# Moving the first pass over a quantised block from ScalarE to VectorE, with new orders for all engines

## The chip, the cores and the metric

The kernel runs on one core of a Trainium2 chip. Time is device time in microseconds (us). The engines are TensorE (PE in the rows), VectorE (DVE), ScalarE (ACT), GpSimd (POOL), and SyncE (SP), which only issues DMAs here. A repeated run of this kernel gave 1418.02 to 1421.85 us.

## The reference

x is (4, 2048, 512) in f32, the context (4, 77, 512). What is computed, cut to what matters:

```python
x = x + tanh(g_xattn[0]) * xattn(layernorm(x), ctx, ctx, mask, Wq, Wk, Wv, Wo)   # 16 heads of 32, 77 keys
x = x + tanh(g_ffn[0]) * ffn(layernorm(x), w_gate, w_up, w_down)                 # 512 -> 2048 -> 512

def act_quant(x):      # per token
    scale = 127.0 / clip(max(abs(x), axis=-1), 1e-5)
    return clip(round(x * scale), -128, 127) / scale
def weight_quant(w):   # ternary
    scale = 1.0 / clip(mean(abs(w)), 1e-5)
    return clip(round(w * scale), -1, 1) / scale
def bitlinear(x, w): return act_quant(x) @ weight_quant(w).T
ffn = lambda x: bitlinear(silu(bitlinear(x, w_gate)) * bitlinear(x, w_up), w_down)
```

## The kernel before

The 8192 tokens are worked on in 16 blocks of 512, each of four tiles of 128. Work is cut into pieces with names such as `F:gu12`: a part (the letter), a step, a tile (or half) and a number in it. The parts run side by side on different blocks. In a repeated round for block g, `A` is the attention of block g, `N` and `Q` are the first layer norm and the q product of block g+1, `F` is the feed-forward net of block g-1, and `E` the end of that of g-2. `W` is the preparation of the weights, in the front alone, with `M` and `R` for block 0's norm and q.

The order of the pieces on each engine is written out by hand in strings: `TENSOR_`, `SCALAR_`, `VECTOR_`, `POOL_` and `SYNC_`, each with `_FIRST` (the front), `_ORDER` (the repeated round) and `_LAST` (the end). `turn` walks through a string and calls the piece's function. Each engine runs its pieces strictly in that order, and semaphores between engines do the rest. So a piece that waits holds up all that stands behind it on its engine.

The feed-forward net for a tile t, step by step:

- `gu` on TensorE (line 1199): gate and up product for one of four column blocks of 512 into two banks; on ScalarE a tanh of the gate (line 739); on VectorE (1 + tanh) times the gate (line 1014); on GpSimd that times `up` (line 607). `up` on ScalarE copies the up product out of its bank (line 747).
- `hm` on VectorE: the largest magnitude of a column block (line 1020). `hs`: six operations on 128x1 that make the scales (lines 1027 to 1032).
- `hq` (line 751, ScalarE): the first pass over the 128x2048 tile, times the scale plus a large number, which rounds. `hb` (line 757, ScalarE): the second pass, minus that number, to bf16. `tH` on the queue of SyncE transposes it by DMA, and `down` on TensorE (line 1211) multiplies it; `down` on VectorE (line 1038) adds x, and a bank is free again.

In the attention, `sc` on TensorE (line 1142) gives scores of five row groups per half; ScalarE takes the exponential twice, to f32 and f16 (lines 707, 708), and GpSimd their difference, the low part (line 598). `pv` (lines 1163 to 1166) is the product with the values, `al` and `ah` the split of it, `wo` (lines 1069 to 1071) the output product, `st`, `zn`, `za` the second layer norm and its scale, `l1` and `l2` its newton steps on GpSimd (lines 563 to 569). In `N`, `xn` normalises (line 938) and `xl` makes the low part (line 943); in `Q`, `q` is the product and its split (line 947 the low part), `s` the maxima of a head's scores (lines 1115 and 953), `mT` their transpose, and `m` on the queue the mask and maxima rows that the scores need.

In `W`, `ws` sums magnitudes on ScalarE, `wm` reduces them over partitions on GpSimd (line 573) and makes the mean, `wu` and `wc` on VectorE clip and round a 128x2048 quarter (lines 913, 919), `wt` on ScalarE writes it as ternary. `w` on the queue loads the next matrix into the quarter that `wt` has read. There are three matrices with four quarters each. The second layer norm's tile lies where the quarters lay, so `A:zn00` waits for all twelve.

Of the kernel before, what the change touches and what calls it, by code (L numbers as in the profile page):

```python
# [11 lines left out]
TT = GT // P  # L12
# [18 lines left out]
def spans(c):  # L31
# [17 lines left out]
MAGIC = 1.5 * 2.0 ** 23  # L49
# [11 lines left out]
    F:gu00 F:gu01 F:gu02 A:sc00 A:sc01 F:gu03 F:gu10 A:sc02 E:down30 A:sc03 A:sc04 F:gu11 F:gu12 A:sc10 F:gu13  # L61
    A:pv00 A:pv01 A:sc11 F:gu20 A:sc12 A:pv02 A:sc13 F:down00 A:sc14 A:pv03 F:gu21 F:gu22 A:pv10 A:pv11 F:gu23
    A:pv12 A:pv13 F:gu30 A:wo00 A:wo10 Q:q00 Q:q10 Q:q20 Q:q30 A:wo20 Q:s00 F:down10 Q:s01 A:wo30 Q:s10 F:gu31
# [3 lines left out]
    F:gu00 E:hq30 F:up00 F:gu01 E:hb30 F:up01 F:gu02 F:up02 F:gu03 A:sc00 F:up03 F:gu10 A:sc01 F:up10 A:sc02  # L67
    F:hq00 A:sc03 F:gu11 A:sc04 F:up11 F:gu12 F:hb00 F:up12 F:gu13 A:sc10 A:sc11 A:ah00 A:ah01 F:up13 A:sc12
    F:gu20 A:ah02 N:xh00 A:sc13 A:sc14 N:xh10 F:up20 F:gu21 A:ah03 F:gu22 F:up21 A:ah10 F:gu23 F:up22 N:xh20
    A:ah11 N:xh30 A:ah12 F:hq10 Q:q00 F:hb10 F:gu30 Q:q10 F:up23 F:up30 A:ah13 A:zq00 A:zb00 Q:q20 Q:q30 A:zq10  # L70
    F:hq20 F:hb20 F:gu31 F:up31 A:zb10 A:zq20 A:zb20 F:gu32 F:gu33 F:up32 F:up33 A:zq30 A:zb30 Q:mT00
"""
VECTOR_ORDER = """
    F:gu00 F:gu01 F:hm00 F:gu02 F:gu03 F:hm01 F:hm02 F:hm03 F:gu10 F:hs00 E:down30 F:gu11 F:gu12 N:ln00 A:pv00
    A:pv01 F:gu13 A:al00 A:al01 N:xn00 N:xn10 A:pv02 F:gu20 F:hm10 F:down00 A:al02 F:hm11 A:pv03 N:xl00 N:xl10
    F:gu21 A:al03 A:pv10 A:pv11 A:al10 F:hm12 N:xn20 F:gu22 N:xl20 A:al11 N:xn30 A:pv12 N:xl30 A:al12 F:hm13
    F:hs10 A:wo00 A:pv13 F:gu23 A:st00 F:hm20 F:hm21 A:wo10 A:st10 Q:q00 F:hm22 A:zn00 A:za00 Q:q10 F:hm23
    F:hs20 Q:q20 A:zn10 Q:q30 F:gu30 A:al13 A:za10 A:wo20 A:st20 Q:s00 F:hm30 F:down10 Q:s01 A:zn20 A:za20
    A:wo30 Q:s10 A:st30 Q:s11 F:gu31 Q:s20 F:gu32 A:zn30 F:gu33 Q:s21 Q:s30 F:hm31 A:za30 F:hm32 Q:s31 Q:mh00
    F:hm33 F:hs30 F:down20  # L80
# [106 lines left out]
def gated_cross_attention_and_ternary_ffn(nc, x, ctx4, mask_keys, mask_cols, mask_rows, gates, wqT, wkT, wvT, woT,  # L187
# [3 lines left out]
    ALU, ACT, AX = mybir.AluOpType, mybir.ActivationFunctionType, mybir.AxisListType  # L191
# [6 lines left out]
    with ctx:  # L198
# [48 lines left out]
        h = region[:, 0:2 * FF].rearrange("p (u n) -> p u n", u=2)  # L247
        hT = region[:, 2 * FF:3 * FF].bitcast(bf16).rearrange("p (u k n) -> p u k n", u=2, k=FK)

        hb = sb("hb", [P, FF], bf16)  # L250
# [1038 lines left out]
```

## Time and profile before

| | |
|---|---|
| median of 3 runs | 1420.9 us (1418.02 to 1421.85) |
| the profiled execution | 1424.24 us, span 1422.4 us, mean granted clock of TensorE 0.958 |
| TensorE busy | 1294.4 us (91%) |
| VectorE busy | 1122.4 us (79%) |
| ScalarE busy | 971.0 us (68%) |
| GpSimd busy | 718.3 us (50%) |

The profiled execution is one of its own, so sums made from its trace are made against its time. An engine's busy time is a mean over stages; the stages here are the front (no feed-forward product yet, to 154.5 us), the repeated rounds, and the end from 1297 us.

### The profile page before, as it was taken

How to read it: one execution, taken by the hardware profiler on the slowest of the kernel's cores; microseconds unless marked ns; L12 is line 12 of the kernel's file. 1: busy time of each engine (PE TensorE's matmuls, PEld its weight loads, DVE VectorE, ACT ScalarE, POOL GpSimd, SP SyncE). 2: the span in 40 equal slices, each digit the busy share in tenths (PEclk: the TensorE clock that was granted, in tenths of full speed). 3: DMA queues.
4: the chain of work that ended last, by engine and by line, in shares of the span. 5: the costliest groups of instructions: out<-in, count | busy, mean ns of one | idle time of the engine just before them, and what ended most of it. 6: DMA issues, size and time to landing. Idle time of an engine off the chain costs nothing.

```text
span 1422.4 us, 25997 instructions
## 1 busy us (share of the span) xinstructions
PE 1294.4 (91%) x7424; PEld 636.9 (45%) x7998; DVE 1122.4 (79%) x2577; ACT 971.0 (68%) x1404; POOL 718.3 (50%) x1187
## 2 busy tenths in 40 slices
PE   5748899999999999999999999999999999999996
PEld 2214344545444454544444454544445454444542
DVE  6978588887968697796969789696878879697784
ACT  4765666768586766858576675958667585857874
POOL 2033354647364563746455464735546473645552
PEclk8867899999999999999999999999999999999999
DMA  8763446464553637354463636346463644536332
GB/s 303 238 205 76 117 86 159 101 150 108 137 132 85 161 83 166 92 150 106 97 173 85 166 92 152 99 112 154 84 164 100 151 104 124 131 81 152 76 77 78
DMA packets 386616, 181.63 MB, mean 128 GB/s; under 512 B 324147, under 2 KB 357811, under 8 KB 384947
## 3 DMA queue, kind: packets, MB, share of 16 engines
q1 hardware_dynamic: 386560, 181.04, 50.8%
q14 instruction: 40, 0.33, 0.1%
q8 instruction: 16, 0.26, 0.1%
HBM read 61.64 MB, written 35.46 MB: 68 GB/s over the span
## 4 chain that ended last, share of the span: by engine, by line
PE 42%; DVE 26%; issue 11%; ACT 9%; POOL 6%; DMA 4%; SPq 1%; ACTq 0%; POOLq 0%; DVEq 0%
PE bank L1211 11%; PE bank L1199 9%; PE bank L1069 7%; PE bank L1070 6%; PE bank L1071 6%; DVE xh L943 4%; DVE xn L938 4%; DVE nmax L953 3%; DVE hmx L1020 2%; ACT up L747 2%; DMA xT<-xh 2%; POOL region L607 2%; DVE region L1014 2%; DVE ah L977 2%; DVE at L971 2%
## 5 line engine op out<-in xcount | busy, mean ns | idle before, releaser
L607 POOL TENSOR_TENSOR region<-region,up 128x512 f32<-128x512 f32 x256 | 336.4, 1322 | 236.7 <-ACT up L747 133.5
L1014 DVE SCALAR_TENSOR_TENSOR region<-region,bank 128x512 f32<-128x512 f32 x256 | 174.4, 682 | 149.2 <-ACT region L739 148.9
L1199 PE MATMUL bank<-tern_gate,region 128*128 128x512 fp8e4 x1024 | 264.5, 381 | 23.5 <-DVE o L1038 14.4
L1199 PE MATMUL bank<-tern_up,region 128*128 128x512 fp8e4 x1024 | 263.2, 379 | 0.0
L1211 PE MATMUL bank<-tern_down,region 128*128 128x512 fp8e4 x1024 | 252.4, 404 | 8.2 <-DMA region<-hb 6.3
L598 POOL TENSOR_TENSOR work<-work 124x512 f16<-124x512 f32 x160 | 195.7, 1237 | 34.3 <-ACT work L708 34.3
L739 ACT ACTIVATE region<-bank,fs 128x512 f32<-128x512 f32 x256 | 180.3, 706 | 47.4 <-PE bank L1199 45.1
L1020 DVE TENSOR_REDUCE hmx<-region 128x1 f32<-128x512 f32 x256 | 170.6, 677 | 38.7 <-POOL region L607 37.8
L751 ACT ACTIVATE region<-region,fs 128x2048 f32<-128x2048 f32 x64 | 127.8, 1996 | 52.5 <-DVE fs L1031 52.5
L1211 PEld LDWEIGHTS bank<-tern_down,region 128*128 128x128 bf16 x1024 | 103.7, 103 | 123.9 <-issue 28.1
L747 ACT ACTIVATE up<-bank 128x512 f32<-128x512 f32 x256 | 154.7, 618 | 4.2 <-PE bank L1199 3.8
L563 POOL TENSOR_TENSOR rs<-mv,lnc 128x1 f32<-128x1 f32 (+1 forms) x80 | 15.3, 192 | 236.5 <-DVE mv L988 220.2
L1199 PEld LDWEIGHTS bank<-tern_up,region 128*128 128x128 bf16 x1024 | 99.0, 97 | 78.7 <-issue 1.1
L757 ACT ACTIVATE hb<-region 128x2048 bf16<-128x2048 f32 x64 | 122.8, 1918 | 0.8 <-DMA region<-hb 0.4
L1199 PEld LDWEIGHTS bank<-tern_gate,region 128*128 128x128 bf16 x1024 | 91.6, 97 | 70.1 <-issue 0.5
L1142 PE MATMUL bank<-q_stack,k_stack 128*128 128x512 f16 x384 | 107.3, 388 | 16.1 <-DMA q_stack<-mT 8.4
L707 ACT ACTIVATE work<-bank,con 124x512 f32<-124x512 f32 x160 | 116.1, 725 | 7.2 <-PE bank L1142 4.4
L708 ACT ACTIVATE work<-bank,con 124x512 f16<-124x512 f32 x160 | 117.3, 733 | 0.0
L953 DVE TENSOR_REDUCE nmax<-bank 128x4 f32<-128x308 f32 x256 | 109.8, 468 | 3.9 <-PE bank L1115 3.3
L722 ACT ACTIVATE region<-region,fs 128x512 f32<-128x512 f32 x64 | 46.2, 723 | 93.8 <-DVE fs L1007 93.7
L1069 PE MATMUL bank<-xT,wq_hi 128*128 128x512 f16 x256 | 97.8, 382 | 9.6 <-DMA xT<-xh 6.9
L1069 PE MATMUL bank<-wo_hi,aT 128*128 128x512 f16 x256 | 98.2, 384 | 6.2 <-issue 5.0
(142 smaller groups left out, 2447.1 us busy)
## 6 DMA issues: line engine op xcount, KB each, us to landing
q_stack<-q_rows SPq DMA_DIRECT2D x96, 256.0 KB, 5.1
xbig<-in_x SPq DMA_DIRECT2D x16, 1024.0 KB, 5.4
q_rows<-q SPq DMA_DIRECT2D x64, 256.0 KB, 2.8
out_y<-o SPq DMA_DIRECT2D x64, 256.0 KB, 2.6
q_stack<-mT SPq DMA_DIRECT2D x32, 256.0 KB, 4.0
region<-in_wgT SPq DMA_DIRECT2D x4, 1024.0 KB, 14.0
region<-in_wuT SPq DMA_DIRECT2D x4, 1024.0 KB, 6.4
region<-in_wdT SPq DMA_DIRECT2D x4, 1024.0 KB, 5.8
```

What stands on the lines that cost most here:

```text
L598: nc.gpsimd.tensor_tensor(p_lo[0:CR, at, :], p32[0:CR, at % PSLOTS, :], p_hi[0:CR, at, :], ALU.subtract).then_inc(p_lo_ready, 1)
L607: nc.gpsimd.tensor_tensor(ht, ht, up[:, n % 2, :], ALU.mult).then_inc(hmul_ready, 1)
L739: nc.scalar.activation(h[:, t % 2, n * GT:(n + 1) * GT], pb[2 * (n % 2)][:, :], ACT.Tanh, scale=fs[:, t, CG:CG + 1]).then_inc(tanh_ready, 1)
L747: nc.scalar.activation(up[:, n % 2, :], pb[2 * (n % 2) + 1][:, :], ACT.Copy).then_inc(up_ready, 1)
L751: nc.scalar.activation(h[:, t % 2, :], h[:, t % 2, :], ACT.Copy, bias=MAGIC, scale=fs[:, t, HSC:HSC + 1]).then_inc(hq_ready, 1)
L757: nc.scalar.activation(hb[:, :], h[:, t % 2, :], ACT.Copy, bias=-MAGIC).then_inc(hb_ready, 1)
L953: V.tensor_reduce(nmax[:, t, HC * cc:HC * (cc + 1)], pb[6 + cc % 2][:, 0:SROWS].rearrange("p (h n) -> p h n", h=HC), AX.X, ALU.max, negate ...
L1014: V.scalar_tensor_tensor(ht, ht, 1.0, pb[2 * (n % 2)][:, :], ALU.add, ALU.mult).then_inc(silu_ready, 1)
L1020: V.tensor_reduce(hmx[:, t % 2, n:n + 1], ht, AX.X, ALU.max, apply_absolute_value=True).then_inc(hmax_ready, 1)
L1069: T.matmul(dst, a_hi_, b_hi_, start=first, stop=False)
L1199: ins = T.matmul(pb[2 * (n % 2) + w][:, :], xqT[:, k, tok], tern[w][:, k * FF + n * GT:k * FF + (n + 1) * GT], start=(k == 0), stop=(k == ...
L1211: ins = T.matmul(pb[2][:, :], hT[:, t % 2, k, :], tern[2][:, k * GT:(k + 1) * GT], start=(k == 0), stop=(k == FK - 1))
```

## The change

The first pass `hq` moves from ScalarE to VectorE: one `tensor_scalar` with multiply and add instead of one activation. Its wait stays the same one, for the scale, and its reader `hb` stays on ScalarE. All 15 order strings are written anew. They were made under the rule that VectorE's two-operand work and GpSimd exclude each other. All other functions stay as they are. The code and, of the strings, the first line of the repeated round of two engines:

```diff
-SCALAR_ORDER = """
-    F:gu00 E:hq30 F:up00 F:gu01 E:hb30 F:up01 F:gu02 F:up02 F:gu03 A:sc00 F:up03 F:gu10 A:sc01 F:up10 A:sc02
+SCALAR_ORDER = """
+    F:gu00 F:up00 E:hb30 F:gu01 F:up01 F:up02 F:gu02 A:sc00 A:sc01 F:gu03 A:sc02 F:gu10 F:up03 A:sc03 A:sc04
-VECTOR_ORDER = """
-    F:gu00 F:gu01 F:hm00 F:gu02 F:gu03 F:hm01 F:hm02 F:hm03 F:gu10 F:hs00 E:down30 F:gu11 F:gu12 N:ln00 A:pv00
+VECTOR_ORDER = """
+    E:hq30 F:gu00 F:gu01 F:hm00 F:gu02 F:hm01 F:hm02 F:gu03 F:hm03 F:gu10 F:hs00 E:down30 F:hq00 A:pv00 A:pv01
...
                     act.wait_ge(hmul_ready, k - 2)
                 nc.scalar.activation(up[:, n % 2, :], pb[2 * (n % 2) + 1][:, :], ACT.Copy).then_inc(up_ready, 1)
-            def hq(f, t, _):
-                act.wait_ge(hscale_ready, f * TT + (t + 1))
-                nc.scalar.activation(h[:, t % 2, :], h[:, t % 2, :], ACT.Copy, bias=MAGIC,
-                                     scale=fs[:, t, HSC:HSC + 1]).then_inc(hq_ready, 1)
-
             def h_integers(f, t, _):
                 act.wait_ge(hq_ready, f * TT + (t + 1))
                 act.wait_ge(hT_in[(t + 1) % 2], f * 32 + 16 * ((t + 1) // 2) + 16)
                 nc.scalar.activation(hb[:, :], h[:, t % 2, :], ACT.Copy, bias=-MAGIC).then_inc(hb_ready, 1)
             pieces = {"Q": {"q": q, "mT": m_high}, "A": {"sc": sc, "ah": a_high, "zq": z_quant, "zb": z_integers}, "N": {"xh": x_high},
-                      "F": {"gu": gu, "up": up_copy, "hq": hq, "hb": h_integers},
+                      "F": {"gu": gu, "up": up_copy, "hb": h_integers},
                       "W": {"tn": gates_tanh, "oh": head_rows, "wh": projection_high, "kh": key_high, "vh": value_high,
                             "ws": weight_sum, "wt": weight_ternary}}
             pieces["M"], pieces["R"] = pieces["N"], pieces.get("Q")
...
                 V.tensor_tensor(at(HSC), at(HRC), at(KAP), ALU.mult).then_inc(hscale_ready, 1)
                 V.tensor_tensor(at(HOUT), at(HAQ), c(OUT0), ALU.mult).then_inc(hout_ready, 1)
+            def hq(f, t, _):
+                dve.wait_ge(hscale_ready, f * TT + (t + 1))
+                V.tensor_scalar(h[:, t % 2, :], h[:, t % 2, :], fs[:, t, HSC:HSC + 1], MAGIC, ALU.mult, ALU.add).then_inc(hq_ready, 1)
+
             def output(f, t, _):
                 dve.wait_ge(hout_ready, f * TT + (t + 1))
                 dve.wait_ge(down_mm, f * TT + (t + 1))
...
                       "A": {"pv": normalise, "al": a_low,
                             "wo": residual, "st": ln2_tile, "zn": z_norm_tile, "za": z_amax},
                       "N": {"ln": ln1, "xn": norm_tile, "xl": x_low},
-                      "F": {"gu": gu, "hm": h_amax, "hs": h_scale, "down": output},
+                      "F": {"gu": gu, "hm": h_amax, "hs": h_scale, "hq": hq, "down": output},
                       "W": {"hc": clear_scalars, "hd": masks, "wx": projection_max, "wp": projection_scale, "wl": projection_low, "km": keys_masked,
                             "kp": key_scale, "kc": key_low, "vm": values_masked, "vp": value_scale, "vc": value_low,
                             "es": score_scale, "ys": output_scale, "wm": weight_mean, "wu": weight_upper, "wc": weight_lower}}
```

The queue's string in the front moves too: block 0's x is the first transfer instead of the eighth, block 1's x is sent before any ternary matrix, and the third matrix (`w20` to `w23`) stands behind `R:m00` instead of ahead of it. On TensorE the front's end is now `q`, `wo` and `s` in turns instead of all `wo`, all `q`, all `s`.

Three places in detail. First GpSimd in the front, from the first reduction on, before. A row `ISA` with no operands is a change of the loaded GpSimd code; with `con<-con` it is a reduction over partitions.

```order
L545 ISA
L545 ISA con<-con 128x1 [waits wmax_ready]
L549 ISA con<-con 128x1 [waits kmax_ready]
L573 ISA con<-con 128x1 [waits wsum_ready]
L553 ISA con<-con 128x1 [waits vmax_ready]
L545 ISA con<-con 128x1 [waits wmax_ready]
L573 ISA con<-con 128x1 [waits wsum_ready] x2
L563 ISA
L563 TENSOR_TENSOR rs<-mv,lnc 128x4 [waits ln1_stats]
```

And now the piece from the last reduction of the first group (line numbers are the same here):

```order
L573 ISA con<-con 128x1 [waits wsum_ready]
L563 ISA
L563 TENSOR_TENSOR rs<-mv,lnc 128x4 [waits ln1_stats]
...
L569 TENSOR_TENSOR rs<-rs 128x4 [waits rstd1_step]
L573 ISA
L573 ISA con<-con 128x1 [waits wsum_ready]
L598 ISA
L598 TENSOR_TENSOR work<-work 124x512 [waits p_hi_ready,exp_ready] x10
L573 ISA
L573 ISA con<-con 128x1 [waits wsum_ready]
L563 ISA
```

Before, the reductions of all three matrices stood in one piece, so the code was changed twice. Now the second block's newton steps stand between the first and the second mean, the ten low parts of p between the second and the third, and the code is changed six times.

Second, VectorE at the end of the front, before: the q product's low parts, then all the maxima, then their split for the transpose.

```order
L996 TENSOR_SCALAR region<-xbig,mv,rs 128x512 [waits zb_ready,ln2_rstd]
L1004 TENSOR_REDUCE fs<-region 128x1 [waits z_norm]
L1005 TENSOR_SCALAR fs<-fs 128x1 [waits dve_quant]
L1007 RECIPROCAL fs<-fs 128x1 [waits ln2_scale]
L947 SCALAR_TENSOR_TENSOR q<-bank,q 128x512 [waits q_hi_ready] x2
L953 TENSOR_REDUCE nmax<-bank 128x4 [waits s_mm] x16
L963 TENSOR_SCALAR mhl<-nmax 128x4x16 [waits mT_mm,smax_ready]
L964 SCALAR_TENSOR_TENSOR mhl<-nmax,mhl 128x4x16 [waits dve_loop]
L1014 SCALAR_TENSOR_TENSOR region<-region,bank 128x512 [waits tanh_ready] x2
```

And now, from the third low part of q on (line numbers are lower by 5 here: 948 is 953 of before, 976 is 981):

```order
L942 SCALAR_TENSOR_TENSOR q<-bank,q 128x512 [waits q_hi_ready]
L914 TENSOR_SCALAR region<-region 128x2048 [waits wupper_ready]
L942 SCALAR_TENSOR_TENSOR q<-bank,q 128x512 [waits q_hi_ready]
L980 BN_STATS st<-xbig 128x6 [waits x2_ready]
L982 MEMSET con 128x1 [waits ln2_halves]
L983 BN_AGGR mv<-st 128x2
L976 SCALAR_TENSOR_TENSOR xbig<-bank,con,xbig 128x512 [waits wo_mm]
L948 TENSOR_REDUCE nmax<-bank 128x4 [waits s_mm] x2
L972 TENSOR_TENSOR ah<-at,ah 128x256 [waits ah_ready]
L980 BN_STATS st<-xbig 128x6 [waits x2_ready]
L982 MEMSET con 128x1 [waits ln2_halves]
L983 BN_AGGR mv<-st 128x2
```

The maxima (`nmax`) now stand two at a time between output products' residuals (`xbig<-bank`), statistics and the last rounds of the weights, and 10 of the 24 passes `wu` and `wc` stand behind the first `pv` where 3 did.

Third, VectorE from the end of one round into the next, before: scales and output of the last tile but one, then the gate products and maxima of the next block.

```order
L1031 TENSOR_TENSOR fs<-fs 128x1 [waits dve_ffn]
L1032 TENSOR_TENSOR fs<-fs,con 128x1
L1038 SCALAR_TENSOR_TENSOR o<-bank,fs,xbig 128x512 [waits out_free0,down_mm,hout_ready]
L1014 SCALAR_TENSOR_TENSOR region<-region,bank 128x512 [waits tanh_ready] x2
L1020 TENSOR_REDUCE hmx<-region 128x1 [waits hmul_ready]
L1014 SCALAR_TENSOR_TENSOR region<-region,bank 128x512 [waits tanh_ready] x2
L1020 TENSOR_REDUCE hmx<-region 128x1 [waits hmul_ready] x3
L1014 SCALAR_TENSOR_TENSOR region<-region,bank 128x512 [waits tanh_ready]
L1027 TENSOR_REDUCE fs<-hmx 128x1 [waits hmax_ready,ffn_scalars]
```

And now:

```order
L1026 TENSOR_TENSOR fs<-fs 128x1 [waits dve_ffn]
L1027 TENSOR_TENSOR fs<-fs,con 128x1
L1037 SCALAR_TENSOR_TENSOR o<-bank,fs,xbig 128x512 [waits out_free0,down_mm,hout_ready]
L1031 TENSOR_SCALAR region<-region,fs 128x2048 [waits hscale_ready]
L1009 SCALAR_TENSOR_TENSOR region<-region,bank 128x512 [waits tanh_ready] x2
L1015 TENSOR_REDUCE hmx<-region 128x1 [waits hmul_ready]
L1009 SCALAR_TENSOR_TENSOR region<-region,bank 128x512 [waits tanh_ready]
L1015 TENSOR_REDUCE hmx<-region 128x1 [waits hmul_ready] x2
L1009 SCALAR_TENSOR_TENSOR region<-region,bank 128x512 [waits tanh_ready]
L1015 TENSOR_REDUCE hmx<-region 128x1 [waits hmul_ready]
L1009 SCALAR_TENSOR_TENSOR region<-region,bank 128x512 [waits tanh_ready]
```

The pass `region<-region,fs` is new at the head of the round, directly ahead of the first gate product. A second one stands behind the next tile's scales and output. The other two of a round stand ahead of the first and behind the last low part of q.

## Rows read from the trace of the kernel before

**Rows 1.** The page: busy us (share of the span) xinstructions; TensorE in 40 slices.

```profile
PE 1294.4 (91%) x7424; PEld 636.9 (45%) x7998; DVE 1122.4 (79%) x2577; ACT 971.0 (68%) x1404; POOL 718.3 (50%) x1187
PE   5748899999999999999999999999999999999996
```

**Rows 2.** Busy time by stage; last, one repeated block. Columns as in the first line.

```profile
core 0: us, PE busy (x) PEld busy (x) DVE busy (x) ACT busy (x) POOL busy (x), PEclk, DMA share, GB/s
0.00:154.50 154.50, 96.36 (x401) 42.77 (x403) 121.94 (x231) 85.10 (x97) 38.82 (x83) 0.76 0.67 206
154.50:1297.00 1142.50, 1086.15 (x6417) 539.65 (x6916) 920.82 (x2164) 796.51 (x1188) 618.24 (x1019) 0.98 0.51 123
1297.00:1422.00 125.00, 111.86 (x609) 54.50 (x680) 79.66 (x183) 89.42 (x119) 61.27 (x85) 0.97 0.32 78
...
915.30:997.04 81.74, 78.17 (x462) 38.81 (x497) 65.92 (x155) 57.11 (x87) 44.24 (x74) 0.98 0.51 123
```

**Rows 3.** What TensorE waited for, 915.30 to 997.04 us: us, times, longest.

```profile
PE bank L1115 <- DVE nmax L953: 1.3, 2, 1.1
PE bank L1199 <- DVE o L1038: 0.9, 1, 0.9
PE bank L1199 <- DVE region L1014: 0.6, 2, 0.4
PE bank L1069 <- DMA xT<-xh: 0.4, 1, 0.4
```

**Rows 4.** TensorE around the last maxima: start us, us, engine, operation.

```profile
881.88 0.69 PE L1115 MATMUL bank<-k_max,q 128*128 128x308 f16 x2 [1.13 <-DVE nmax L953]
883.36 5.31 PE L1211 MATMUL bank<-tern_down,region 128*128 128x512 fp8e4 x16
...
899.29 3.62 PE L1211 MATMUL bank<-tern_down,region 128*128 128x512 fp8e4 x16
```

**Rows 5.** The chain of waits, longest pieces: first and last slow down product.

```profile
474.25 5.22 PE bank L1211 x16
...
1292.88 5.21 PE bank L1211 x16
```

**Rows 6.** Groups by line and form: busy us, mean ns, idle before, releaser.

```profile
L607 POOL TENSOR_TENSOR region<-region,up 128x512 f32<-128x512 f32 x256 | 336.4, 1322 | 236.7 <-ACT up L747 133.5 <-DVE region L1014 101.7 <-ACT work L708 1.4
...
L751 ACT ACTIVATE region<-region,fs 128x2048 f32<-128x2048 f32 x64 | 127.8, 1996 | 52.5 <-DVE fs L1031 52.5
...
L943 DVE TENSOR_TENSOR xh<-xn,xh 128x512 f16<-128x512 f32 x64 | 73.6, 1167 | 4.4 <-ACT xh L680 2.6
```

**Rows 7.** VectorE in order of time: rounds alone, with GpSimd busy; a low part alone.

```profile
34.08 1.28 DVE L913 TENSOR_SCALAR region<-region,con 128x2048 f32<-128x2048 f32 x1
35.27 1.22 DVE L919 TENSOR_SCALAR region<-region 128x2048 f32<-128x2048 f32 x1
...
100.10 4.27 DVE L913 TENSOR_SCALAR region<-region,con 128x2048 f32<-128x2048 f32 x2
...
850.33 0.69 DVE L943 TENSOR_TENSOR xh<-xn,xh 128x512 f16<-128x512 f32 x1
```

**Rows 8.** VectorE at the start of a block.

```profile
893.47 0.69 DVE L1014 SCALAR_TENSOR_TENSOR region<-region,bank 128x512 f32<-128x512 f32 x1 [2.27 <-ACT region L739]
...
896.34 0.69 DVE L1014 SCALAR_TENSOR_TENSOR region<-region,bank 128x512 f32<-128x512 f32 x1 [1.34 <-ACT region L739]
```

**Rows 9.** VectorE in the front.

```profile
12.92 2.47 DVE L925 BATCH_NORM_STATS2 st<-xbig 128x6 f32<-128x512 f32 x4 [0.26 <-DMA xbig<-in_x]
...
95.45 1.35 DVE L938 TENSOR_SCALAR xn<-xbig,mv,rs 128x512 f32<-128x512 f32 x1 [7.44 <-POOL rs L569]
...
145.41 7.99 DVE L953 TENSOR_REDUCE nmax<-bank 128x4 f32<-128x308 f32 x16
```

**Rows 10.** TensorE, the first scores.

```profile
88.35 3.40 PE L1142 MATMUL bank<-q_stack,k_stack 128*128 128x512 f16 x7 [7.88 <-DMA q_stack<-mT]
```

**Rows 11.** GpSimd in the front: first reduction, first newton step behind the reductions.

```profile
24.73 0.66 POOL L545 PARTITION_ALL_REDUCE con<-con  x1 [6.07 <-issue]
...
92.69 0.19 POOL L563 TENSOR_TENSOR rs<-mv,lnc 128x4 f32<-128x4 f32 x1 [6.97 <-issue]
```

**Rows 12.** ScalarE at the end: the last first pass and the last second pass.

```profile
1405.95 2.00 ACT L751 ACTIVATE region<-region,fs 128x2048 f32<-128x2048 f32 x1 [1.46 <-DVE fs L1031]
1408.32 1.91 ACT L757 ACTIVATE hb<-region 128x2048 bf16<-128x2048 f32 x1 [0.36 <-DMA region<-hb]
```

## What I expected before the change was run

> **What bounds the kernel now.** I read the page first (busy time by engine, the 40 slices), then busy time by stage, then what TensorE waits for in one repeated block, then single instructions around the longest of those waits. TensorE is busy 91% of the span and 9 tenths or more in nearly every slice but the first four [rows 1]. By stage [rows 2]: up to 154.5 us, where the first feed-forward product starts, it is busy 96.4 us, so 58.1 us are idle; from there to 1297 us it is busy 1086.2 of 1142.5, 56.3 idle; in the last 125 us, 13.1 idle. The middle is fourteen blocks of 512 tokens, about 81.7 us each. In one of them TensorE is busy 78.17, VectorE 65.92, ScalarE 57.11 and GpSimd 44.24 of 81.74 us [rows 2]. So the middle is TensorE's, with at most 81.74 - 78.17 = 3.6 us to win per block, and the front belongs to the other engines and the queue. TensorE's named waits in that block are 1.3 (the maxima), 0.9 (the output that empties a bank), 0.6 (the gate product) and 0.4 us (a transpose): 3.2 us [rows 3]. Where it waits for the maxima it stands 1.13 us, and behind that the `down` product takes 5.31 us instead of 3.62: its clock is at the lower of its two levels there, 1.2 GHz and not 2.4 [rows 4], which costs 1.7 us. The chain of waits shows such a `down` of 5.2 us in eleven of the fourteen blocks, the first at 474.25 and the last at 1292.88 [rows 5].
>
> **The change, part by part.** My sum is made against the profiled execution, 1424.24 us with a span of 1422.4; the median of the runs shown is 1420.9, 3.3 less, so I take every term off the median.
>
> *The first pass.* Line 751 leaves ScalarE: 64 times 1996 ns, 8.0 us per block [rows 6]. VectorE gets 64 `tensor_scalar` operations of 128x2048 f32. Its nearest rows are the same operation in the weight preparation: 1.28 us alone, with the next one starting 1.19 behind it, and 4.27 us for two when GpSimd runs, so 2.14 each [rows 7]. That is 4.8 to 8.5 us per block. VectorE then has 70.7 to 74.4 of 81.74 us. What hides it is its idle time of 15.8 us per block. Two of the four passes land at a block's start, where VectorE waits 2.27 and 1.34 us for ScalarE's tanh, which stood behind the old first pass [rows 8]; that cover grows, since the tanh comes earlier. The other two (tiles 1 and 2) stand right ahead of the first low part of q and right behind the last. There VectorE has no such gaps. By my count the low part of the second q product is ready half a us before TensorE needs it for the fourth; a pass at 2.14 instead of 1.19 uses that up.
>
> I take the lower end for the two passes at a block's start and the middle for the other two, 2 x 1.19 + 2 x 1.67 = 5.7 us.
>
> The Trainium skill says more of this ("SBUF — State Buffer", section "Who interferes with whom"): a VectorE operation in a two-port mode and a GpSimd instruction exclude each other for the whole of an instruction, whoever starts first. The two prices above agree. By that rule alone, with GpSimd busy half of the time, each pass costs near the middle of the two prices and GpSimd's products are held up as well. It would make 6.6 us of the four passes, and it speaks against the change.
>
> *The loop's new order.* I followed the new order through one block with durations of the trace. Three of the old waits should go: the output's 0.9 (that operation now stands ahead of its reader by more than a us), the gate product's 0.6 (ScalarE is 8 us freer) and the transpose's 0.4 (its last normalised tile is issued one product earlier): 1.9 us. Against them stand: the first `down` of a block waits for the integer pass, which ScalarE has behind six score operations (about 0.8); the second maxima of tile 1 (0.2); and the last two maxima, where VectorE is later by about one pass (1.3 grows to 2.2): 1.9 us. Net zero, with 1 us per block, 14 us in all, open on both sides.
>
> *The front.* Four waits go or shrink. (a) VectorE's statistics start at 12.92 when x lands [rows 9], because x is the eighth transfer; it is now the first. The newton steps then start earlier, but GpSimd must have its code; 2.7 us. (b) The first scores stand 7.88 us for the mask rows until 88.35 [rows 10], issued on the queue behind a third set of weights (4 MB); the mask rows are now issued ahead of those weights: 5 us. (c) VectorE stands 7.44 us until 95.45 for the second block's newton steps [rows 9], which sat on GpSimd behind the last reduction; it is now far ahead: 7.4 us. (d) The 16 maxima that close the front take 7.99 us on VectorE, two at a time with TensorE [rows 9]; now they alternate with the `wo` products: 4 us. Against: (e) the weights' clip and round passes are put off. Behind the first normalised tile stood 3 of 24, now 10: seven more at 1.19 to 2.14, 8.3 to 15.0; I take 9. (f) GpSimd has four more code changes. Between a newton step and a reduction it stands 6.07, and back 6.97 us, "issue" in the view [rows 11]; in the program each such place has one ISA row, two such changes of before become six. Four times 6.5 is 26 us of GpSimd, bound to its own queue. Two lie where GpSimd waits anyway, since the row itself waits for nothing and so starts early; the one ahead of the low parts of p and the one ahead of the third weights' mean can show. From nothing to 26; I take 2, since that queue has nothing else to do between the reduction and the first low part. Front: -2.7 - 5 - 7.4 - 4 + 9 + 2 = -8.1.
>
> The Trainium skill names the cause ("GPSIMD Engine Reference", section "Instruction dispatch"): "The first call to a freshly-loaded kernel additionally pays an IRAM-load of approximately 6 µs". The rows have 6.07 and 6.97. If only the first load of each kernel paid, the 6.97 of the way back would not be there, so the trace is for a price at every change; by the page the four extra would cost nothing or 24.
>
> *The tail.* The last first pass takes 2.00 on ScalarE, and the integer pass behind it waits another 0.36 for the transfer of the tile before [rows 12]. On VectorE it is 1.28, and the integer pass of the tile before is now earlier: -1.1.
>
> Sum: -8.1 + 0 - 1.1 = -9.2, so 1415.0 for a profiled execution and 1411.7 for the median; I say 1411.5.
>
> **The rivals.**
> *Clean loop.* The old waits go and no new one comes, 1.9 us x 14 = 27; with the idle time before the slow `down` shorter its lower clock may go too (1.7 us in eleven blocks). 1420.9 - 9 - 27 = 1385, a few us less with the clock. For it: 8 us less ScalarE per block and 3.2 us of wait in many small pieces. Against: TensorE's largest wait is a chain of product and maximum that no order shortens.
> *VectorE becomes the bound (slower).* Place: from the last gate product of tile 3 to the last maxima. Passes meet GpSimd at 2.14 each, VectorE has 74.4 of 81.7 us, and the low parts of q and the maxima come 1.2 to 2.2 us later than I have them in each block: 14 x 1.2 - 9 = 8, 1429, up to 14 x 2.2 - 9 = 22, 1443. It decides from 0.95 us per block on: 14 x 0.95 = 13.3 takes the gain of 9 and 0.3% more. For it: 91% of VectorE in order; contended rows already show 1167 ns for an operation that takes 0.69 us alone [rows 6, 7]. Against: the new order may have fewer such meetings.
> *The code changes come onto the path.* Two show in full, 13 less 2: 1411.5 + 11 = 1422, no change.
> *The orders do not do what they say.* GpSimd's product stays at 1322 ns and line 943 at 1167 [rows 6]: the loop is as before and the front's terms cancel: 1420.
>
> **How the numbers follow.** Forecast 0.43 (1411.5, own range 1403 to 1418), clean loop 0.19 (1385 to 1402), VectorE the bound 0.19 (1425 to 1443), code changes 0.12, orders without effect 0.07. A measurement of this kernel tells 0.3% from nothing, 4.3 us: faster is under 1416.6, slower over 1425.2. Nine tenths of the forecast's lower three quarters, all of the clean loop and a little of the rest: faster 0.60; same: the forecast's upper part and most of the two last: 0.20; slower 0.20. The range reaches from 1391 to 1430: it leaves out the far end of the clean loop and of the slower case.
>
> **What would show it.** VectorE's new row at about 1.3 to 1.8 us in the mean and 64 times; ScalarE's busy time 128 us less; the first feed-forward product at about 146 us instead of 154.5, with two gaps near 7 us of "issue" on GpSimd before the low parts of p and none longer than 3 us on VectorE; blocks of 80.7 to 82.7 us; in a block no wait of TensorE for an output, and a longer one for the maxima; the last integer pass right behind the last first pass. The prediction is wrong if blocks leave that band (a us per block is 14 us in all), if the front is not shorter by 4 us at least, or if TensorE waits in the q products.

## The result, and the profile after

The changed kernel takes 1372.3 us (median; 1370.4 to 1373.2) against 1419.5 for the kernel before in the same runs. The ratio is 0.967 (0.964 to 0.969), 47 us less. The prediction said 1411.5, from 1391 to 1430: the direction was right, and the time lies far outside the range. The profiled execution took 1373.2 us with a span of 1371.4.

The page, TensorE's clock in 40 slices, busy time in the same three stages as in [rows 2], and one repeated block:

```profile
PE 1267.3 (92%) x7424; PEld 632.0 (46%) x7998; DVE 1153.7 (84%) x2641; ACT 864.8 (63%) x1340; POOL 737.6 (54%) x1187
...
PEclk9868899999999999999999999999999999999999
```

```profile
0.00:147.90 147.90, 91.13 (x400) 41.02 (x402) 112.44 (x225) 82.50 (x93) 37.95 (x77) 0.81 0.77 212
147.90:1239.00 1091.10, 1061.49 (x6411) 535.62 (x6911) 952.32 (x2218) 707.33 (x1135) 635.38 (x1025) 1.00 0.55 129
1239.00:1371.40 132.40, 114.63 (x617) 55.35 (x687) 88.96 (x200) 74.98 (x112) 64.26 (x85) 0.96 0.32 76
...
615.92:693.61 77.69, 75.96 (x461) 38.34 (x497) 68.33 (x160) 50.57 (x81) 45.27 (x74) 1.00 0.59 134
```

The middle has got 51 us shorter, half of it idle time of TensorE (56.3 to 29.6 us) and half busy time at nearly the same number of recorded products (1086.2 to 1061.5 us). A block takes 77.7 us instead of 81.7 [rows 2]. What TensorE waits for in that block, and its last maxima and the `down` behind them:

```profile
PE bank L1114 <- DVE nmax L948: 1.0, 2, 0.8
PE bank L1068 <- DVE q L942: 0.6, 1, 0.6
```

```profile
614.45 0.69 PE L1114 MATMUL bank<-k_max,q 128*128 128x308 f16 x2 [0.77 <-DVE nmax L948]
615.33 0.69 PE L1114 MATMUL bank<-k_max,q 128*128 128x308 f16 x2 [0.19 <-DVE nmax L948]
615.92 3.63 PE L1210 MATMUL bank<-tern_down,region 128*128 128x512 fp8e4 x16
```

Against [rows 3] the waits for the output, the gate product and the transpose are gone, and one in the q products is new. Against [rows 4] the wait for the maxima is 0.77 instead of 1.13 us and the `down` takes 3.63 us, in this block and in all fourteen: no lower clock in the loop. The groups of VectorE and GpSimd that answer to [rows 6, 7]:

```profile
L1031 DVE TENSOR_SCALAR region<-region,fs 128x2048 f32<-128x2048 f32 x64 | 81.9, 1280 | 0.0
...
L938 DVE TENSOR_TENSOR xh<-xn,xh 128x512 f16<-128x512 f32 x64 | 43.4, 696 | 4.6 <-ACT xh L680 4.5
...
L933 DVE TENSOR_SCALAR xn<-xbig,mv,rs 128x512 f32<-128x512 f32 x64 | 33.4, 544 | 0.1
```

The new first pass never meets GpSimd: 1280 ns is the price alone. And two groups that nobody touched are cheaper: the low part of normalised x, 1167 ns before, takes 696, and the normalisation, 928 before, 544. That is (471 + 384) x 4 = 3.4 us per block, while the four passes add 5.1. So VectorE's block is 68.3 us, and not the 71.0 that 65.9 and 5.1 would make. Where they run now, GpSimd has a pause (GpSimd first, then VectorE):

```profile
650.11 1.26 POOL L607 TENSOR_TENSOR region<-region,up 128x512 f32<-128x512 f32 x1
660.78 0.54 POOL L563 TENSOR_TENSOR rs<-mv,lnc 128x1 f32<-128x1 f32 x1 [9.41 <-DVE mv L983]
```

```profile
652.74 0.99 DVE L933 TENSOR_SCALAR xn<-xbig,mv,rs 128x512 f32<-128x512 f32 x2
...
654.05 1.29 DVE L938 TENSOR_TENSOR xh<-xn,xh 128x512 f16<-128x512 f32 x2
```

In the kernel before, GpSimd was busy 10.1 of 10.8 us there, and the same pairs took:

```profile
915.30 2.65 DVE L938 TENSOR_SCALAR xn<-xbig,mv,rs 128x512 f32<-128x512 f32 x2 [0.37 <-POOL rs L569]
...
921.79 2.35 DVE L943 TENSOR_TENSOR xh<-xn,xh 128x512 f16<-128x512 f32 x2
```

My theory after this comparison: the order carries the gain, because it puts these eight VectorE operations of a block into a pause of GpSimd; the move of the pass is affordable only in that order; and the clock adds what the shorter waits give back. The rival: ScalarE's 8 us per block are the gain, and any order would have it.

### The profile page after: what moved, and what is told of

Read it like the earlier page. It is cut to its first block, busy times and chain, and to the rows that moved or that the text cites. A ratio compares the mean times of both kernels' runs of the same rounds, so it can differ in the third digit from the quotient of the medians.

```text
span 1371.4 us, 26005 instructions
## 1 busy us (share of the span) xinstructions
PE 1267.3 (92%) x7424; PEld 632.0 (46%) x7998; DVE 1153.7 (84%) x2641; ACT 864.8 (63%) x1340; POOL 737.6 (54%) x1187
## 4 chain that ended last, share of the span: by engine, by line
PE 59%; DVE 28%; DMA 4%; issue 4%; ACT 4%; POOL 1%; SPq 1%; POOLq 0%; ACTq 0%; DVEq 0%
PE bank L1198 20%; PE bank L1210 16%; PE bank L1141 5%; DVE region L1009 5%; DVE nmax L948 4%; PE bank L1068 4%; PE bank L1070 4%; PE bank L1069 4%; DVE xh L938 3%; DVE xbig L976 2%; DVE xn L933 2%; DVE hmx L1015 2%; DVE st L980 2%; DMA region<-hb 2%; PE bank L1114 1%
## 5 line engine op out<-in xcount | busy, mean ns | idle before, releaser
L607 POOL TENSOR_TENSOR region<-region,up 128x512 f32<-128x512 f32 x256 | 344.9, 1350 | 135.1 <-DVE region L1009 84.6
L1210 PE MATMUL bank<-tern_down,region 128*128 128x512 fp8e4 x1024 | 233.2, 382 | 12.2 <-DMA region<-hb 11.5
L739 ACT ACTIVATE region<-bank,fs 128x512 f32<-128x512 f32 x256 | 177.4, 697 | 92.1 <-PE bank L1198 91.7
L563 POOL TENSOR_TENSOR rs<-mv,lnc 128x1 f32<-128x1 f32 (+1 forms) x80 | 26.5, 331 | 292.8 <-DVE mv L983 283.0
L1210 PEld LDWEIGHTS bank<-tern_down,region 128*128 128x128 bf16 x1024 | 97.7, 98 | 108.1 <-issue 1.9
L1141 PE MATMUL bank<-q_stack,k_stack 128*128 128x512 f16 x384 | 103.4, 392 | 15.3 <-DMA q_stack<-mT 10.0
L1068 PE MATMUL bank<-xT,wq_hi 128*128 128x512 f16 x256 | 98.5, 385 | 10.0 <-DVE q L942 8.4
L717 ACT ACTIVATE ah<-at 128x256 f16<-128x256 f32 x128 | 55.1, 431 | 82.4 <-DMA aT<-ah 45.8
L688 ACT ACTIVATE q<-bank 128x512 f16<-128x512 f32 x64 | 38.0, 593 | 97.4 <-PE bank L1070 97.3
L1069 PE MATMUL bank<-xT,wq_hi 128*128 128x512 f16 x256 | 98.2, 384 | 0.0
```

What stands on the lines that cost most here:

```text
L607: nc.gpsimd.tensor_tensor(ht, ht, up[:, n % 2, :], ALU.mult).then_inc(hmul_ready, 1)
L739: nc.scalar.activation(h[:, t % 2, n * GT:(n + 1) * GT], pb[2 * (n % 2)][:, :], ACT.Tanh, scale=fs[:, t, CG:CG + 1]).then_inc(tanh_ready, 1)
L1068: T.matmul(dst, a_hi_, b_hi_, start=first, stop=False)
L1069: T.matmul(dst, a_hi_, b_lo_, start=False, stop=False)
L1141: ins = T.matmul(pb[4 + at % 2][:, :], k_stack[:, lo:lo + P], q_stack[:, HH * hf + h_, :], start=(i == 0), stop=(i == len(SPANS[cc]) - 1))
L1210: ins = T.matmul(pb[2][:, :], hT[:, t % 2, k, :], tern[2][:, k * GT:(k + 1) * GT], start=(k == 0), stop=(k == FK - 1))
```

## Experiments

"Block" below is the distance between two like `down` products in the profile.

### The two halves of the change

e1: the pass on VectorE, all else as before. e2: the new orders, the pass on ScalarE.

```
e1, VECTOR_ORDER:  F:hs00 -> F:hs00 F:hq00   (so for each tile; hq gone from SCALAR_ORDER)
e2, SCALAR_ORDER:  A:ah01 -> A:ah01 F:hq00   F:hb20 -> F:hq20 F:hb20   (hq gone from VECTOR_ORDER)
```

> The first pass stands on VectorE right behind the scale of its tile; everything else keeps the old orders. If the gain is that of ScalarE's 8 us per block (theory A), the loop gets shorter by itself: 1385 to 1400 us. If the gain is that of the new order and the pass alone only loads VectorE (theory B), the waits for outputs (13.3 us) and products (8.1 us) stay or grow, the slow `down` stays, and the time is 1415 to 1440 us.

> The new orders of all engines, but the first pass is back on ScalarE, close ahead of the integer pass of its tile. Theory A: ScalarE's 8 us per block are back and so are the waits: 1410 to 1425 us. Theory B: the order carries the gain and ScalarE has the room: 1372 to 1388 us.

Measured: e1 1460.1 us, ratio 1.029 (1.024 to 1.035); e2 1409.1, ratio 0.992 (0.990 to 0.994). One block of each:

```profile
569.60:653.00 83.40, 77.59 (x462) 38.15 (x499) 71.47 (x160) 49.71 (x81) 45.22 (x75) 1.00 0.48 121
```

```profile
545.70:625.60 79.90, 76.48 (x461) 38.30 (x497) 64.68 (x156) 58.02 (x85) 43.34 (x74) 1.00 0.51 125
```

And e1's waits of TensorE in all, with its pass:

```profile
PE bank L1198 <- DVE o L1037: 34.9, 34, 2.0
...
PE bank L1068 <- DVE at L966: 15.1, 14, 1.4
```

```profile
L1031 DVE TENSOR_SCALAR region<-region,fs 128x2048 f32<-128x2048 f32 x64 | 96.1, 1501 | 0.0
```

The pass alone costs about 40 us, the orders alone gain about 11, both together gain 47. ScalarE's 8 us as the whole gain are out: e1 has them and is slower, with the pass at 1501 ns. But "the order carries the gain" was too simple too: I expected 1372 to 1388 of e2. Nor is the pause enough: in e2, too, the normalisation takes 544 ns and the low part 696, TensorE waits 0.77 us for the maxima and no `down` of the loop is slow, and still its blocks take 80.0 us and not 77.7; in the one above TensorE waits 1.3 us for gate products and 1.0 for a low part of p. So with these orders and places the pass costs 2.3 us more per block on ScalarE than on VectorE. The loop shows it best: a block takes 80.2 us before with a normal `down` (e11, below), about 83.4 with the pass alone, 80.0 with the orders alone and 77.7 with both. So the gain of the loop belongs to the pair, an order made for VectorE with the pass and ScalarE without. What e2 gains on the kernel before is not its loop's: the front alone gives as much (e4, below). I chose e2's places for the pass, and the end shows it: TensorE waits 17.8 us in all for low parts of p and 14.4 for the integers' transpose, and from the last `down` of the loop to the end e2 takes 141.0 us against 133.4 in the change. That orders with the pass on ScalarE can't do better is not shown.

### Front and loop

e3: the change with the old strings of the front. e4: the kernel before with the new ones.

```
e3:  after.py with TENSOR_FIRST ... SYNC_FIRST of before.py;   e4: the reverse
```

> The changed kernel with the old orders up to the first feed-forward product. By the stages of the two profiles the front is worth 6.6 us and the loop the rest: the first feed-forward product at about 154.5 us and 1379 us in all. If the new front also sets how the loop runs (phase of the engines when it starts), more comes back: 1390 us or more.

> The kernel before with only the new orders of the front. The first feed-forward product at about 148 us, blocks unchanged at 81.6 us: 1413 us. If the front's gain is lost behind it: 1419 us.

Measured: e3 1378.7, ratio 0.972 (0.967 to 0.977); e4 1409.6, ratio 0.993 (0.990 to 0.996). The first `down` of the old loop starts at 180.8, 178.8 and 182.6 us with the old front (before, e11, e8) and at 173.2 with the new one (e4); that of the new loop at 186.7 with the old front (e3) and at 180.6, 177.8 and 178.1 with the new one (after, e16, e5). By these means the front is worth 7.5 to 7.9 us, but each has a single profile on one side, and profiles with the same front differ by up to 6 us. The other measures surround it: the medians of e3 and of the change are 6.4 us apart, e4's ratio makes 9.5 us (with its share of the clock), and the first feed-forward product starts at 151.5 to 156.2 us in the five profiles with the old front and at 142.1 to 147.9 in the twelve with the new one. e3's blocks are 77.7 us, e4's 80.2: the loop's gain doesn't hang on the front.

### Is it GpSimd's pause?

e6 fills the pause with seven products per block that nobody reads.

```
+                if t == 1 and n == 3 and (not isinstance(f, int) or f == 0):
+                    for i in range(7): ...
+                        nc.gpsimd.tensor_tensor(scratch[:, :], wq_hi[:, 0, :], wq_hi[:, 1, :], ALU.mult)
```

> The changed kernel, with seven more products of 128x512 f16 per block on GpSimd, into a tile that nobody reads, in the pause of 9.4 us in which VectorE's eight tiles of x norm and its low part now run (ordinary work is not displaced if they fit the pause). If what the new order wins is that these eight meet no GpSimd, their means rise from 544 and 696 ns towards the old 928 and 1167, VectorE is 2 to 3.5 us later per block, and a part of it reaches TensorE: 1380 to 1415 us. If the exclusion of the two engines has no part in the gain, the time stays within 3 us of 1372.

Measured: 1451.5 us, ratio 1.021 (1.019 to 1.022): 79 us more than the change, above my range. VectorE's rows and TensorE's in one block:

```profile
L944 DVE TENSOR_TENSOR xh<-xn,xh 128x512 f16<-128x512 f32 x64 | 70.1, 1111 | 2.3 <-ACT xh L686 2.2
L939 DVE TENSOR_SCALAR xn<-xbig,mv,rs 128x512 f32<-128x512 f32 x64 | 66.2, 1054 | 0.1
```

```profile
609.13 1.89 PE L1204 MATMUL bank<-tern_gate,region 128*128 128x512 fp8e4 x4 [4.64 <-DVE region L1015]
```

This is shown: with GpSimd busy at that place, both groups are back at 1.05 to 1.11 us, VectorE is busy 72.8 us per block instead of 68.3, TensorE waits 4.6 us in this block behind VectorE (61.2 us in the whole run), and its clock then falls for some products (1.89 us for four gate products instead of 1.04). GpSimd's own work isn't pushed back by the extra products: after the seven it stands idle for another 5.3 us until VectorE's next statistics. It costs 79 us over fourteen blocks, 5.6 us each, more than the whole gain of the change.

### The slow `down`

e8 moves one step in the kernel before; e11 is that kernel once more; e9 (below) lengthens the wait.

```
e8, VECTOR_ORDER:  F:gu33 Q:s21 -> Q:s21 F:gu33
```

> The kernel before with one step moved: on VectorE the maxima of the last pair of tile 2 stand ahead of the last gate product of tile 3. TensorE's wait for the maxima shrinks from 1.13 to about 0.5 us: 9 us in all, 1412 us, and the gate product 0.8 us later costs nothing. If the shorter wait also spares the slow `down`, up to 19 us more: 1395 us. If the gate product is late for the next block, no change: 1420 us.

> The kernel before, once more, for its profile. The first profile has eleven slow `down` products of 5.2 us in the loop and one in the tail; the run with only a new front, whose loop has the same order and the same waits of 1.13 us, had one in the loop. If the slow products depend on something that differs from run to run, their number is another one here and the time goes with it by 1.7 us each; if they belong to the order, there are eleven again and 1424 us.

Measured: e8 1410.8, ratio 0.992 (0.990 to 0.993); e11's single execution 1407.9. e8's waits are 0.53 and 0.68 us instead of 1.13 and 0.19: moved, not removed, and its blocks with a normal `down` take 80.1 us as e11's do (80.2). The rest is the number of slow `down` products. Of the fourteen last maxima with their `down` in the loop, eleven are slow in the first profile of before, two in e11 and one in e4, all with waits of 1.13 and 0.19 us; five in e1 (1.19 and 0.19) and two in e8 (0.53 and 0.68). None is in after, e2, e3, e5, e13, e14 and e16 (0.77 and 0.19), nor in e12 (0.44 and 0.7). A block of e11 against the slow one in [rows 2]:

```profile
553.90:634.10 80.20, 76.75 (x461) 38.40 (x497) 65.82 (x156) 57.06 (x85) 44.25 (x74) 1.00 0.52 125
```

With a wait of 1.1 us the clock falls in some executions and blocks and not in others. Each time it makes about 1.5 us, so the nine more in the first profile of before than in e11 are 14 of their 16 us; most of the spread of before (1408 to 1426 us) may be this. That e8 is better than the median of before can be this alone; whether its step changes the odds stays open.

### A delay ahead of the maxima, and 16 bytes

e7 was meant to put three extra maxima on VectorE in every block; they stood in the first block only. e9 has them in every block, e10 in the ninth.

```
+                    if t == 2 and cc == 2 and g == 2:        # e9: g >= 2; e10: g == 9
+                        for i in range(3): ... V.tensor_reduce(scratch[:, :], pb[6][...], ...)
```

> The changed kernel with three more maxima of 128x308 on VectorE, into a tile that nobody reads, ahead of the second maxima of tile 2: TensorE's wait ahead of the last two products grows from 0.77 to about 2.1 us in every block. The wait alone is 1.3 us in 14 blocks, 1391 us. If a longer wait there also brings the slow `down` back (5.2 instead of 3.5 us), 1.7 more per block: 1410 to 1416 us, and rows of 5.2 us in the chain.

> The three extra maxima of the run before last stood in the first block only, and yet every later block took 79.4 instead of 77.7 us: one delay of 1.4 us cost 23 us in all. Here they stand in each of the fourteen blocks. Theory C (the loop has a second way of running, in which a first pass meets GpSimd, and once in it stays there): the extras cost nothing more than their own 1.3 us or less per block on top, 1400 to 1418 us. Theory D (VectorE is the bound of the loop from the maxima on, so that each delay there shows in full and is never made good): 1.4 us x 14 on 1372, 1392 us, and e7's 1400 would be chance.

> The changed kernel with the three extra maxima in the ninth block alone (near 770 us). Theory C: blocks of 77.7 us up to there and of 79.4 behind it, six of them: 1372 + 6 x 1.7 = 1382 to 1384 us. Theory D: one delay of 1.4 us, 1373.5 us, blocks of 77.7 us on both sides.

Measured: e7 1400.5, ratio 0.985 (0.983 to 0.987); e9 1432.9, ratio 1.009 (1.006 to 1.013); e10 1401.2, ratio 0.987 (0.983 to 0.990). All of my theories fell: e10 has blocks of 79.4 us from the second one on, 500 us ahead of its delay. In e9 the wait is 2.18 us in every block, and the `down` behind it is slow in thirteen of the fourteen. One of them, and the first block, where it is not:

```profile
555.62 1.83 PE L1121 MATMUL bank<-k_max,q 128*128 128x308 f16 x4 [2.18 <-DVE nmax L955]
557.25 4.70 PE L1217 MATMUL bank<-tern_down,region 128*128 128x512 fp8e4 x16
```

```profile
225.31 0.69 PE L1121 MATMUL bank<-k_max,q 128*128 128x308 f16 x2 [2.18 <-DVE nmax L955]
226.19 0.69 PE L1121 MATMUL bank<-k_max,q 128*128 128x308 f16 x2 [0.19 <-DVE nmax L955]
226.72 3.62 PE L1217 MATMUL bank<-tern_down,region 128*128 128x512 fp8e4 x16
```

So a longer wait makes the lower clock more frequent, and no wait here decides it alone: never behind 0.77 us, in one to eleven of fourteen blocks behind 1.1 to 1.2, in thirteen of fourteen behind 2.18. The second wait counts as well, since two `down` products of e8 were slow with 0.53 and 0.68 us. What e7, e9 and e10 share besides are 16 bytes of memory per partition, which shift every later tile, and a semaphore. e13 and e14 add these alone.

```
e13: +        scratch = sb("scratch", [P, 4], f32)
e14: +        extra = sem("extra")
```

> The changed kernel with 16 bytes per partition of on-chip memory reserved behind the wide keys' tile and used by nobody, so that every later tile lies 16 bytes higher. The run with a delay in the ninth block had blocks of 79.4 us from the second one on, long before its delay, so theories C and D in their first form both fell: something that this kernel shares with the one of the delay in the first block, and not the delay, puts the loop into the slower way. Those two share the 16 bytes and one more semaphore. If it is the 16 bytes: blocks of 79.4 us, a mean of the first pass of 1465 to 1480 ns, 1398 to 1402 us. If not: 77.7, 1280 ns and 1372 us.

> The changed kernel with one more semaphore reserved ahead of all the others and used by nobody. If the slower way comes from it: 79.4 us per block and 1398 to 1402 us. If not: 77.7 us per block and 1372 us. If both this one and the 16 bytes run at 77.7, the extra maxima in a block of their own are needed and the cause stays open.

Measured: e13 1396.7, ratio 0.987 (0.983 to 0.992), blocks of 79.4; e14 1369.5, ratio 0.967 (0.963 to 0.971), blocks of 77.7. It is the 16 bytes. Since e9 and e10 have them too, only a part of their time over the change belongs to their delay (e9's blocks are 82.0 us, e10's 79.4). The trace shows how the 16 bytes act. The transfers into the shifted tiles take longer (median us from issue to landing, after, then e13):

```profile
q_stack<-mT SPq DMA_DIRECT2D x32, 256.0 KB, 4.1
...
xT<-xh SPq DMA_TRANSPOSE x64, 2.8
```

```profile
q_stack<-mT SPq DMA_DIRECT2D x32, 256.0 KB, 4.7
...
xT<-xh SPq DMA_TRANSPOSE x64, 3.3
```

For the 30 us up to one operation of ScalarE, 46 us into a block, the two programs agree to about 0.02 us (0.5 us that ScalarE loses earlier at another transpose are made good by then). It waits for such a transfer, and VectorE's pass comes 21 us behind it. After:

```profile
648.67 0.42 ACT L717 ACTIVATE ah<-at 128x256 f16<-128x256 f32 x1 [0.96 <-DMA aT<-ah]
...
669.41 1.29 DVE L1031 TENSOR_SCALAR region<-region,fs 128x2048 f32<-128x2048 f32 x1
```

e13, where the block lies 6.4 us later in time:

```profile
655.77 0.42 ACT L718 ACTIVATE ah<-at 128x256 f16<-128x256 f32 x1 [1.67 <-DMA aT<-ah]
...
676.54 2.26 DVE L1032 TENSOR_SCALAR region<-region,fs 128x2048 f32<-128x2048 f32 x1
```

ScalarE is 0.7 us late, VectorE with it, and its pass is no longer ahead of GpSimd's next product but behind it: 2.26 instead of 1.29 us. TensorE's wait in the q products is then 1.7 to 1.8 us instead of 0.6, in twelve of the fourteen blocks; in the first and the ninth the pass takes 1.29 us and the wait is 0.5 and 0.3. This is shown. Why the shifted tiles take longer to fill is not: e6 shifts the same tiles by 1024 bytes, and its transfers land in 4.1 us (`q_stack<-mT`) as in the change.

### The tail, and a better version

e5: the old strings behind the loop, the pass still on VectorE. e12: e5 with two steps moved. e15: two gate products ahead of the last block's first scores. e16: the change again, beside e15.

```
e12, VECTOR_ORDER:  F:hq10 Q:q00 -> Q:q00 F:hq10    F:gu33 Q:s21 -> Q:s21 F:gu33
e15, TENSOR_LAST:   A:sc00 F:gu00 A:sc01 A:sc02 F:gu01 -> F:gu00 F:gu01 A:sc00 A:sc01 A:sc02
```

> The changed kernel, but behind the last repeated block the old orders, with each first pass right behind its scale on VectorE. From the last `down` of the fourteenth block to the end the changed kernel takes 133 us and the one before 129.5, 1.7 of which is a slow `down`. If the new order of the tail is what is worse, this one is back at 128 to 130 us: 1368 to 1370 us in all. If the tail pays for the passes on VectorE, whatever their order, it is longer than the new one: 1376 us or more, as the run with the passes moved alone (2.5% slower in all) lets one expect.

> The changed kernel with the old order of the tail (1369.5 us) and two steps of VectorE moved in the loop: the low part of the first q product ahead of the first pass that stood before it, and the maxima of the last pair of tile 2 ahead of the last gate product of tile 3. TensorE's waits of 0.6 us in the q products and of 0.77 us for the maxima (1.4 per block, 19 us in all) go: 1352 to 1360 us. If a pass that is 0.6 us later meets GpSimd, or the loop falls into its second way of running, 1385 us or more.

> The changed kernel with one edit behind the loop: the last block's first two gate products stand ahead of its first scores, on TensorE, ScalarE and GpSimd. Behind the loop the changed kernel has one wait of 4.0 us, the first scores for the transposed maxima, that the one before doesn't have; two products of 1.9 us cover it. If the tail's loss (133.4 us from the last `down` of the loop to the end, against 128.3) is that wait: 129.5 us and 1366 to 1369 us in all. If what follows is bound by VectorE and its passes, the wait comes back further on: 133 us and 1370 to 1372 us.

> The changed kernel once more, on the same chip as the edit of its tail, to compare the two there; and with it whether its loop always runs at 77.7 us per block without a slow `down`, as in the first profile: 1368 to 1373 us.

Measured: e5 1369.5 us, ratio 0.963 (0.961 to 0.965); e12 1379.7, 0.971 (0.969 to 0.974); e15 1366.7, 0.961 (0.958 to 0.964); e16 1369.9, 0.964 (0.960 to 0.967). From the last `down` of the loop to the end e5 takes 133.2 us and after 133.4, against 128.3 in e11 and 128.4 in e4: e5's time comes from an earlier start of the loop, not from its tail. So with the pass on VectorE both orders of the tail lose 5 us. After's only long wait there:

```profile
1245.86 0.59 PE L1141 MATMUL bank<-q_stack,k_stack 128*128 128x512 f16 x2 [3.99 <-DMA q_stack<-mT]
```

e15 covers it with 1.9 us of products, and its six timed runs (1364.0 to 1367.2, the middle of them 1366.2) all lie under the six of e16 (1367.6 to 1372.7): about 4 us less, in the range expected, and the fastest version here. Its one profiled execution took 4479 us and its rows are not read, so that the wait itself is gone is not shown. e12 is slower than e5, with blocks of 78.4 us: once per block its pass met GpSimd, and TensorE waits 1.2 us in the q products.

```profile
672.32 1.85 DVE L1031 TENSOR_SCALAR region<-region,fs 128x2048 f32<-128x2048 f32 x1
```

## Why the prediction was wrong, step by step

*The loop at no net gain* is the step that failed. Its removed side held: the output's 0.9, the gate product's 0.6 and the transpose's 0.4 us are gone. Its added side was 1.9 us and came out at about 0.5: the maxima took 1.0 us in all, 0.3 less than before, and not 2.2; the `down` of a block waits 3.0 us in the whole middle (0.2 per block) and not 0.8 each; the q products took 0.6 that I had warned of and not counted. The loop got 48.2 us shorter where I had 0. That the direction came out right is the front's doing, and not this step's.

Two inputs were wrong. The first is the maxima. I had VectorE later by about a pass there. In the kernel before three operations stand ahead of the last four maxima, in the new order two (the kernel before first, then the change):

```profile
879.54 0.69 DVE L1014 SCALAR_TENSOR_TENSOR region<-region,bank 128x512 f32<-128x512 f32 x1
880.14 0.70 DVE L996 TENSOR_SCALAR region<-xbig,mv,rs 128x512 f32<-128x512 f32 x1
880.76 0.68 DVE L1014 SCALAR_TENSOR_TENSOR region<-region,bank 128x512 f32<-128x512 f32 x1
```

```profile
612.70 0.68 DVE L1015 TENSOR_REDUCE hmx<-region 128x1 f32<-128x512 f32 x1
613.32 0.69 DVE L1009 SCALAR_TENSOR_TENSOR region<-region,bank 128x512 f32<-128x512 f32 x1
```

The second is the durations. I walked the new order with the old, contended ones: 1167 ns for the low part [rows 6], though [rows 7] has the same operation at 0.69 alone, and 1.67 as the middle for a pass. In the new order all of these run beside an idle GpSimd, and VectorE is busy 68.3 us per block where I had 65.9 + 5.7 = 71.6. e6 shows what that is worth: 4.5 us more of VectorE per block cost 5.6. How the 31 us without the clock divide between the two inputs was not measured.

*The clock.* The sum put it at nothing; I had it in a rival only, as "a few us", though eleven times 1.7 is 19. Eleven slow products in the profiled execution of before, none in after: ten of them between the first feed-forward product and the last block's `down`, 17 us. Its share differs between executions: e11 had two.

*The ledger*, profile against profile, span 1422.4 to 1371.4. Front 154.5 to 147.9: -6.6 (forecast -8.1). Loop, from there to its last `down`, 1138.3 to 1090.1: -48.2, of which 17 are the clock and 31 waits and shortened products (forecast 0). Tail 129.6 to 133.4: +3.8, or +5 against a before without a slow product (forecast -1.1). Sum -51.

*The front* came out near its sum (142.1 to 147.9 us for the first feed-forward product in twelve profiles, 146 forecast), but not as I described it: VectorE has a wait of 8.8 us at 94.08 for the first p v products, where I said none over 3, and TensorE waits 3.6 us for the low parts of p, ahead of which GpSimd, whose code is changed there, stands 7.18 us. (In the kernel before its waits for them in the front were 2.2 us, so the 2 us in the sum are not refuted.) The four edits in it were not taken apart.

*The first pass* was priced at 1.3 to 1.8 us; 1.28 is the lower end. The Trainium skill's rule ("SBUF — State Buffer", section "Who interferes with whom") is that the one which issues first blocks the other for the whole instruction. e1, where one pass of each block takes 2.15 us and the others 1.28, e6 and e13 (2.26 us) agree with it. From it and GpSimd's busy half I had taken a cost near the middle. Such a mean does not hold where the order of both engines repeats in every block: a meeting happens in nearly every block (each one in e1, twelve of fourteen in e13) or in none (the change).

*The tail* was taken as two operations of ScalarE getting shorter. That the new order puts the first scores ahead of everything (the wait of 3.99 us), and what VectorE's passes cost at the end, where e5 with the old order is as long, was not looked at. The passes as the cause of the rest are argued, not shown.

*The rival "clean loop"* (1385 to 1402) came nearest in its mechanism and had 0.19. Its own range missed too: 1372.3 lies below it, and with the 19 us of the clock its sum is 1366. I held against it that no order shortens product and maximum; it shortened VectorE's path between them.

## What to carry to other kernels

When an order changes, the durations change with it: price a contended operation from a row without the other engine too, and follow both engines' pauses through one period before taking a mean. In a loop whose order is fixed, a meeting of two engines costs its full price in nearly each turn or nothing, so moving an operation and ordering around it have to be judged together (+40, -11, -47 us here). Look at TensorE's clock behind each wait as a term of its own.

## What the runs showed of the hardware

- 16 unused bytes per partition ahead of the tiles cost 27 us: transfers into the shifted tiles landed 0.1 to 0.6 us later (medians), and one VectorE pass lost its turn against GpSimd in twelve of fourteen blocks. 1024 bytes (e6) left the transfers as they were.
- TensorE's clock behind a wait in an otherwise full stretch: not lower after 0.77 us (seven profiles of fourteen blocks), in one to eleven of fourteen blocks after 1.13 to 1.19, in thirteen of fourteen after 2.18, and for some products after 4.64.
- A GpSimd product of 128x512 took nearly as long in f16 as in f32: medians of 1216 and 1269 ns in e6, means of 1296 and 1292.
